# A block of attention and experts on one core: scores in four 32-row tiles, causal masks on TensorE, near values on GpSimd, products with the values in two stretches

## What is computed

```python
scores = jnp.einsum('bhqd,bhkd->bhqk', Qh, Kh)
idx = _rel_index(S, S)            # clip(k - q, -2, 2) + 2
rel_k = rel_k_table[idx]
scores = (scores + jnp.einsum('bhqd,qkd->bhqk', Qh, rel_k)) / scale
causal = jnp.tril(jnp.ones((S, S), dtype=bool))
scores = jnp.where(causal[None, None], scores, -1000000000.0)
attn = jax.nn.softmax(scores, axis=-1)
out = jnp.einsum('bhqk,bhkd->bhqd', attn, Vh)
out = out + jnp.einsum('bhqk,qkd->bhqd', attn, rel_v_table[idx])
x = x + _layernorm(out.transpose(0, 2, 1, 3).reshape(B, S, E) @ W_o + b_o)
```

## Time and profile before

| | us |
|---|---|
| median of 3 runs | 1036.85 |
| lowest, highest | 1036.38, 1038.85 |
| span of the profiled execution | 1036.5 |
| share busy in the span: PE, PEld, DVE, ACT, POOL | 86%, 50%, 80%, 65%, 70% |

### The profile page before, as it was taken

How to read it: one execution, slowest core, us unless ns; L and a number is a source line. 1 busy time by engine, 2 the same in 40 slices (tenths; PEclk the granted TensorE clock), 3 DMA queues, 4 the chain that set the end, 5 groups by cost and what they waited for, 6 DMA issues and landing times. The chain is left out here.

```text
span 1036.5 us, 23477 instructions
## 1 busy us (share of the span) xinstructions
PE 896.3 (86%) x7655; PEld 513.6 (50%) x7655; DVE 833.7 (80%) x1948; ACT 676.3 (65%) x1305; POOL 727.1 (70%) x940
## 2 busy tenths in 40 slices
PE   2778889889889898898898988986679999999995
PEld 0324444444444444444444444432457777777773
DVE  5578888888988888889888888877568788878884
ACT  2038677777676777776777777765447767676773
POOL 4135686876867868768678687576357989898886
PEclk9769999999999999999999999988889999999999
DMA  2610110110101101011011011101425455555441
GB/s 48 170 44 34 35 44 31 47 42 32 49 31 42 45 32 47 32 43 49 32 42 44 33 47 40 35 18 50 148 59 169 144 165 150 169 151 166 162 140 31
DMA packets 64004, 74.93 MB, mean 72 GB/s; under 512 B 10032, under 2 KB 39600, under 8 KB 63904
## 3 DMA queue, kind: packets, MB, share of 16 engines
q1 hardware_dynamic: 61536, 73.17, 22.4%
q10 hardware_dynamic: 2368, 0.48, 0.3%
HBM read 43.75 MB, written 8.65 MB: 51 GB/s over the span
## 5 line engine op out<-in xcount | busy, mean ns | idle before, releaser
L1128 DVE TENSOR_REDUCE mx<-ps_s 128x1 f32<-128x512 f32 (+2 forms) x640 | 408.6, 681 | 84.3 <-PE ps_s L1540 83.7
L799 ACT ACTIVATE prob<-ps_e 128x512 f32<-128x512 f32 x640 | 349.6, 606 | 103.3 <-PE ps_e L1497 103.2
L641 POOL TENSOR_SCALAR_AFFINE_SELECT prob<-prob 128x516 f32<-128x516 f32 (+1 forms) x320 | 174.9, 571 | 141.8 <-ACT prob L799 141.8
L1519 PE MATMUL ps_s<-ks,qs 63*128 63x512 f16 (+3 forms) x1024 | 224.5, 312 | 47.4 <-DVE mx L1128 31.5
L1497 PE MATMUL ps_e<-qs,ks 64*128 64x512 f16 (+3 forms) x1024 | 212.1, 307 | 3.7 <-ACT prob L799 1.7
L721 POOL TENSOR_TENSOR hidden_low<-hidden,hidden_high 128x512 fp32r<-128x512 f32 x144 | 191.1, 1356 | 12.1 <-ACT hidden_high L989 10.9
L1557 PE MATMUL ps_av<-prob,vp 128*32 128x512 f32 (+3 forms) x2048 | 182.4, 452 | 4.3 <-POOL prob L641 4.2
L1519 PEld LDWEIGHTS ps_s<-ks,qs 63*128 63x128 f16 x1024 | 67.6, 95 | 184.0 <-DVE mx L1128 80.5
L989 ACT CAST hidden_high<-hidden 128x512 fp32r<-128x512 f32 x160 | 98.0, 612 | 30.5 <-DVE hidden L1441 27.3
L1540 PE MATMUL ps_s<-masked_at,below_r 64*128 64x128 bf16 (+3 forms) x640 | 103.1, 211 | 0.0
L1540 PE MATMUL ps_s<-masked_at,below 64*128 64x128 bf16 (+3 forms) x640 | 91.3, 213 | 0.0
(11 more groups left out here) (177 smaller groups left out, 1737.7 us busy)
## 6 DMA issues: line engine op xcount, KB each, us to landing
gate_rows<-gates_dram SPq DMA_DIRECT2D x128, 256.0 KB, 3.6
qs<-qh SPq DMA_DIRECT2D x128, 32.0 KB
qs<-ql SPq DMA_DIRECT2D x128, 32.0 KB
xnT_dram<-oT SPq DMA_DIRECT2D x16, 256.0 KB, 2.0
xeT<-xnT_dram SPq DMA_DIRECT2D x16, 256.0 KB, 2.7
out<-result SPq DMA_DIRECT2D x16, 256.0 KB, 2.3
v_near<-v_back SPq DMA_DIRECT2D x16, 254.0 KB
ks<-kh SPq DMA_DIRECT2D x124, 32.0 KB
```

Source lines behind the costliest of these rows:

```text
L641: pool.affine_select(out=v, in_=v, compare_op=ALU.is_ge, fill=0.0, base=-2, pattern=cols, channel_multiplier=-1).then_inc(S["p_masked"], 1)
L799: act.activation(prob[g % 2][:, u, b, :], ps_e[bank][:, :], ACT.Exp, scale=SCALE).then_inc(S["e_done"], 1)
L1128: dve.tensor_reduce(out, src, AX.X, ALU.max).then_inc(s_free[bank], 1)
L1519: pe.matmul(scores[:, at:at + P * (qt + 1)], qs[par][rows, 2 * g + off, P * qt:P * qt + P], ks[par][rows, 2 * g + off, 0:P * (qt + 1)], st ...
```

## The change

- A tile has 32 rows: three products (low-low is gone) of 8 columns at rows 4d, 4d+1, 4d+2, the row 31 for the maxima, and three of the rows 4i+3 for a large negative product that masks the one near key across a boundary of two blocks of 128. TensorE has four tiles. E units of group g use tiles 2(g mod 2) and the next, S units run group g xor 1 and so use the other two.
- The units are cut anew: u = 0 and 3 hold the four diagonal blocks of a head, u = 1, 2 and 4 hold blocks that need no mask. A diagonal unit is four matmuls of 128 columns, and then four mask matmuls of 4 x 32 columns, for S and E alike. GpSimd masks nothing.
- Products with the values: in u = 1 the diagonal blocks of the group before (16 matmuls of 128 columns), in u = 3 the rest (widths 384, 256, 128). They wait for ScalarE's exponents (`e_done`).
- Bank v0 is read by ScalarE alone; GpSimd makes `v_back` and `v_near` from `vp` (`values_near`).
- Three pairs of stack buffers of half the size, six transfers a sequence, all in the step of stage F. One transfer for each half of the maxima in place of two. Other order of heads in `wq` and `wk`, other constants, among them six transfers that turn the mask table.

The diff, cut to its core (removed bodies are left out; they stand in the code above; the piece behind `e_part` is `s_part`):

```diff
-HALF = P // 2
-M_ROW = HALF - 1
+ROWS = 32
+M_ROW = ROWS - 1
+BIG = 65504.0
...
-E_UNITS = [[(0, 0, 0)], [(0, 1, 0), (0, 3, 384)], [(0, 2, 0), (1, 2, 256)], [(1, 0, 0)], [(1, 1, 0), (1, 3, 384)]]
-S_UNITS = [[(0, 3, 0)], [(0, 2, 0), (0, 0, 384)], [(0, 1, 0), (1, 1, 256)], [(1, 3, 0)], [(1, 2, 0), (1, 0, 384)]]
...
+def diagonal(off):
+    return [(off, t, P * t, P * t, P) for t in range(NT)]
+E_UNITS = [diagonal(0), [(0, 0, P, 0, 3 * P), (0, 2, 3 * P, 3 * P, P)], [(0, 1, 2 * P, 0, 2 * P), (1, 1, 2 * P, 2 * P, 2 * P)],
+           diagonal(1), [(1, 0, P, 0, 3 * P), (1, 2, 3 * P, 3 * P, P)]]
+S_UNITS = [diagonal(0), [(0, 3, 0, 0, 3 * P), (0, 1, 0, 3 * P, P)], [(0, 2, 0, 0, 2 * P), (1, 2, 0, 2 * P, 2 * P)],
+           diagonal(1), [(1, 3, 0, 0, 3 * P), (1, 1, 0, 3 * P, P)]]
+DIAGONAL = (0, 3)
...
+AV_AT = {1: ("diagonal",), 3: (0, 1, 2)}
+def row_tile(g, b):
+    return 2 * (g % 2) + b
+def rows_of(tile, n=ROWS):
+    return slice(ROWS * tile, ROWS * tile + n)
...
+            def stacks_out(st, s):
+                if s < 3:
+                    sp.wait_ge(S["k_rows"], 2 * (s + 1))
+                    sp.wait_ge(S["q_rows"], 2 * (s + 1))
+                for stk, parts in ((qs[s % 3], (qh, qh, ql)), (ks[s % 3], (kh, kl, kh))):
+                    if s == 0 and stk is ks[0]:
                         continue
-                    for b in range(2):
-                        for r, part in enumerate(parts):
-                            lo = 64 * b + D * r
-                            src = 64 * b + 32 * half
-                            sp.dma_start(stk[lo:lo + D, prs, :], part[src:src + 32, :]).then_inc(stacks[par][half], 16)
+                    for r, part in enumerate(parts):
...
-            def mask_tiles(st, lo, hi):
-                for g, part in ((i // NU, i % NU) for i in range(lo, hi)):
-                    last = {0: 3, 1: 3, 2: 5, 3: 9, 4: 9}[part]
...
+            def values_near(st):
+                by_head = lambda v: v.rearrange("p t (h d) -> p t h d", d=D)
+                apart = lambda i: dv[:, i, :].rearrange("p (h d) -> p h d", d=D).unsqueeze(1).to_broadcast([P, NT, H, D])
+                v = vp[st.a % 2][:, :, :, 0:D]
+                pool.wait_ge(s_free[st.s_use("v0")[1]], st.s_turn("v0") + 1)
+                need(pool, S["v_shifted"], 32 * st.a)
+                pool.tensor_tensor(by_head(v_back[:, :, :]), v, apart(0), ALU.add).then_inc(S["back_made"], 1)
+                need(pool, S["near_ready"], 4 * st.a)
+                own.mark(pool.tensor_tensor(by_head(v_near[:, 0]), v, apart(1), ALU.add))
             def near_half(st, s, half):
...
-            def values_out(st):
...
             def s_max(st, i):
-                g, u, b = i // (2 * NU), i % (2 * NU) // 2, 1 - i % 2
+                g, u, b = i // (2 * NU) ^ 1, i % (2 * NU) // 2, i % 2
                 n, bank = st.s_use(f"s{i}")
-                scores, (off, qt, _) = ps_s[bank][:, :], S_UNITS[u][0]
-                h = 2 * (2 * g + off) + b
-                if len(S_UNITS[u]) == 1:
-                    out, src = mx[:, QT0 + qt, h:h + 1], scores
+                h, n_seg = 4 * g + 2 * b + S_UNITS[u][0][0], 2 if u == 2 else NT
+                src = ps_s[bank][:, :].rearrange("p (n c) -> p n c", n=n_seg)
+                if u in DIAGONAL:
+                    out = mx[:, 0:TOP + 1:DIAG_AT, h]
                 elif u == 2:
-                    out, src = mx[:, QT0 + qt, h:h + 3:2], scores.rearrange("p (n c) -> p n c", n=2)
+                    out = mx[:, TOP + 8, h:h + 2]
                 else:
-                    out, src = mx[:, 0:QT0 + 1:4, h], scores.rearrange("p (n c) -> p n c", n=NT)
+                    out = mx[:, TOP + 1:TOP + 5, h]
...
-                own.mark(dve.tensor_reduce(mx[:, QT0 + 2, hs], mx[:, 0:QT0:4, hs].rearrange("p r h -> p h r"), AX.X, ALU.max))
+                own.mark(dve.tensor_reduce(mx[:, 3, hs], mx[:, TOP:TOP + 4, hs].rearrange("p r h -> p h r"), AX.X, ALU.max))
+                pairs = mx[:, :, hs].rearrange("p (k r x) h -> p r h k x", k=2, r=3, x=4)[:, 1:3, :, :, 0]
+                own.mark(dve.tensor_reduce(mx[:, 1:3, hs], pairs, AX.X, ALU.max))
...
             def e_part(st, i, scores, n):
                 g, u, b = i // (2 * NU), i % (2 * NU) // 2, i % 2
-                par, rows = st.b % 2, slice(HALF * b, HALF * b + HALF)
-                off, kt, at = E_UNITS[u][n]
-                pr = 2 * g + off
-                last = pe.matmul(scores[:, at:at + WIDTH[kt]], ks[par][rows, pr, P * kt:P * kt + P],
-                                 qs[par][rows, pr, P * kt:SEQ], start=True, stop=True)
-                if n == len(E_UNITS[u]) - 1:
+                rows = rows_of(row_tile(g, b))
+                off, kt, q0, at, w = E_UNITS[u][n]
+                slot = 2 * (g // 2) + off
+                last = pe.matmul(scores[:, at:at + w], ks[st.b % 3][rows, slot, P * kt:P * kt + P],
+                                 qs[st.b % 3][rows, slot, q0:q0 + w], start=(n == 0),
+                                 stop=(u not in DIAGONAL and n == len(E_UNITS[u]) - 1))
+                if u not in DIAGONAL and n == len(E_UNITS[u]) - 1:
                     last.then_inc(S["e_full"], 1)
...
+                g, u, b = i // (2 * NU) ^ 1, i % (2 * NU) // 2, i % 2
+                rows = rows_of(row_tile(g, b), M_ROW)
+                off, qt, k0, at, w = S_UNITS[u][n]
+                slot = 2 * (g // 2) + off
+                last = pe.matmul(scores[:, at:at + w], qs[st.a % 3][rows, slot, P * qt:P * qt + P],
+                                 ks[st.a % 3][rows, slot, k0:k0 + w], start=(n == 0),
+                                 stop=(u not in DIAGONAL and n == len(S_UNITS[u]) - 1))
+                if u not in DIAGONAL and n == len(S_UNITS[u]) - 1:
+                    last.then_inc(S["s_full"], 1)
+            def mask_part(bank, tile, side, part, full):
+                blocks = bank[:, :].rearrange("p (n c) -> p n c", n=NT)[:, :, ROWS * part:ROWS * part + ROWS]
+                columns = masked_at[rows_of(tile), :].unsqueeze(1).to_broadcast([ROWS, NT, ROWS])
+                last = pe.matmul(blocks, tri[rows_of(tile), (part - tile) % 4, side, :], columns,
+                                 start=False, stop=(part == 3))
+                if part == 3:
+                    last.then_inc(full, 1)
+            def av_part(st, s, g, part):
+                par, then = s % 2, st if g < NGRP - 1 else Step(st.t0 - 1)
+                if part == "diagonal":
+                    pe.wait_ge(S["e_done"], then.e_use(f"e{2 * NU * g + 7}")[0] + 1)
+                    need(pe, S["av_copied"], NGRP * s + g)
                     if g == 0:
...
+                        made = Step(st.t0 - 1)
+                        pe.wait_ge(s_free[made.s_use("v0")[1]], made.s_turn("v0") + 1)
+                    for kt in range(NT):
+                        for j in range(4):
+                            pe.matmul(ps_av[32 * j:32 * j + 32, P * kt:P * kt + P], vp[par][:, kt, 4 * g + j, :],
+                                      prob[g % 2][:, DIAGONAL[j % 2], j // 2, P * kt:P * kt + P],
+                                      start=(kt == 0), stop=False)
+                    return
+                pe.wait_ge(S["e_done"], then.e_use(f"e{2 * NU * g + 9}")[0] + 1)
                 for j in range(4):
...
+                    u, at = (2, 2 * P * (j % 2)) if part == 1 else (DIAGONAL[j % 2] + 1, 0 if part == 0 else 3 * P)
+                    w = SEQ - P * (part + 1)
+                    last = pe.matmul(ps_av[32 * j:32 * j + 32, P * (part + 1):SEQ], vp[par][:, part, 4 * g + j, :],
+                                     prob[g % 2][:, u, j // 2, at:at + w], start=False, stop=(part == 2))
+                if part == 2:
                     last.then_inc(S["av_full"], 1)
...
+                    s_banks, e_banks = [None, None], [None, None]
+                    for n in range(len(E_UNITS[u])):
+                        for b in range(2):
+                            if st.A:
+                                if n == 0:
+                                    s_banks[b] = s_unit(st, 2 * r + b)
+                                s_part(st, 2 * r + b, s_banks[b], n)
+                            if st.B:
+                                if n == 0:
+                                    e_banks[b] = e_unit(st, 2 * r + b)
+                                e_part(st, 2 * r + b, e_banks[b], n)
+                    if u in DIAGONAL:
+                        for part in range(4):
+                            for b in range(2):
+                                if st.A:
+                                    mask_part(s_banks[b], row_tile(g ^ 1, b), 0, part, S["s_full"])
+                                if st.B:
+                                    mask_part(e_banks[b], row_tile(g, b), 1, part, S["e_full"])
+                    for part in AV_AT.get(u, ()):
                         if g > 0 and st.B:
...
+                            av_part(st, st.b, g - 1, part)
```

(1 more changed line is left out.)

287 lines of the change are left out of this document (89 added, 198 removed).

## The result

| | before | after |
|---|---|---|
| median, us | 1037.85 (1036.38 to 1039.70) | 1134.61 (1126.89 to 1136.76) |
| span of the profiled execution, us | 1036.5 | 1134.9 |
| TensorE's mean granted clock | 0.960 | 0.844 |
| q matmuls to q matmuls, a step | 41.4 us | 48.0 to 50.7 us |

The changed kernel takes 1.092 times as long (95% interval 1.088 to 1.095). The forecast was 977 us.

The account below looks back on a forecast made before the run. The prediction took a step as VectorE's work plus holes from TensorE's stretches: 35.1 + 2.6 = 37.7 us, 3.7 less, 56 us over 15 steps; with 1.5 and 2 us, 59 off 1036.5 gives 977 us, range 962 to 995 (wider, 950 to 1035).

Parts of the forecast that it names:

- What bounds the kernel: Attention step of 41.41 us: VectorE's 36.03 us of work plus 5.38 us of holes torn by TensorE's stretches.
- VectorE's work: VectorE's own work in a step: 36.03 us less 1.37 plus 0.4, so 35.1 us.
- GpSimd: GpSimd loses its masks, gains the near-value additions, ends near 21.8 us a step and bounds nothing.
- The near values: Two additions moved from VectorE to GpSimd: 0.69 and 0.68 us a step off VectorE's work.
- Four tiles overlap: Scores and exponent scores in four 32-row TensorE tiles run together; a diagonal round's scores and masks take 0.58 us.
- the rival of two tiles: Only two TensorE tiles overlap, holes stay 4.66 us, a step 39.8 us: 1010 us, chance 0.17.
- the one with the starts as the limit: Rival: 654 matmul starts a step limit TensorE, a step is priced at 44 us: 1076 us, chance 0.13.
- TensorE's busy time: Scores and masks on TensorE: 1.5 us less a group, 6 us a step.
- Products with the values: Two TensorE stretches instead of three: -0.1 us a group, set against a larger hole, counted as nothing.
- What reaches the step: VectorE's seven waits a step shorten by 0.3 us each, 2.1 us; holes after, 2.6 us.
- TensorE's clock: TensorE's clock in the steps, 1.00 in five steps; a fall below full was named only as making the forecast wrong.

Follow-up runs that it names:

- order_av3: Changed kernel with products with the values in three stretches, xn2 transposed behind round 18's scores, and the maxima merged two reductions later: 1000.8 us.
- best1: order_av3 plus ten redundant TensorE matmuls a step (four in round 16, three in round 18, three in round 3): 1003.8 us.
- best1_near_dve: best1 with the two additions that make the near values back on VectorE: 1019.4 us.
- order: Changed kernel, still two stretches, with xn2 transposed behind round 18's scores and the first half's maxima merged two reductions later: 1062.3 us.
- before_two: Kernel before with its products with the values in two stretches for a group of heads instead of three, nothing else: 1115.3 us.
- fill_both: Changed kernel with 17 redundant TensorE matmuls a step where it stood idle (round 13, and before xn2's transposes in round 18): 1067.6 us.

## Why the prediction was wrong, point by point

**What bounds the kernel**: right. In every step shown above with stage C in it the length is VectorE's 34 to 36 us of work plus its idle time, most of it waits for TensorE; what differs is the holes.

**VectorE's work**, 35.1 forecast: 34.8 to 34.9 us a step in the windows above, 34.2 in order_av3. **GpSimd**, 21.8: 22.7. Both right. The near values, taken at 1.4 us a step or 22 in all, cost 15.6 on VectorE. At full clock they put 0.93 us on its work and 0.87 on a step (best1, then best1_near_dve):

```profile
314.87:354.34 39.47, 35.27 (x663) 19.82 (x659) 34.23 (x91) 30.34 (x61) 22.72 (x27) 1.00 0.11 36
239.13:279.47 40.34, 35.11 (x660) 19.91 (x659) 35.16 (x93) 30.42 (x61) 20.45 (x25) 1.00 0.11 35
```

**Four tiles overlap**: right. In a diagonal round at full clock (changed kernel, timeline of TensorE) four matmuls start within 10 ns and the next four 50 to 70 ns later, masks too:

```profile
89.67 0.22 PE L1499 MATMUL ps_s<-ks,qs 31*128 31x128 f16 x1
89.67 0.22 PE L1476 MATMUL ps_e<-qs,ks 32*128 32x128 f16 x1
89.73 0.21 PE L1499 MATMUL ps_s<-ks,qs 31*128 31x128 f16 x1
89.73 0.21 PE L1476 MATMUL ps_e<-qs,ks 32*128 32x128 f16 x1
...
89.85 0.22 PE L1509 MATMUL ps_s<-masked_at,tri 32*128 32x128 bf16 x1
89.85 0.21 PE L1509 MATMUL ps_e<-masked_at,tri 32*128 32x128 bf16 x1
```

The first two of the round's 32 matmuls stand before a wait; the other 30 start within 0.41 us (89.66 to 90.07), 14 ns each. The factor of 3.07 in place of 4, which the prediction cited from the Trainium skill ("TensorE: Matmul & The Clock Gate", "Measured speedup vs the span model"), isn't seen here: the sets of four follow each other seven times in 0.41 us, every 58 ns or so, where the prediction took 55 to 60 for a full overlap. The 62 ns for each matmul with hardware decode off (the Trainium skill, "TensorE: Matmul & The Clock Gate", "Wait — 56ns, not 53.3ns?") aren't seen either, at 14. So the rival of two tiles is out, and so is the one with the starts as the limit: it had the right sign (1076 us) for the wrong reason, since it decided from 58 ns a start. TensorE's busy time in a step at full clock fell by 4.3 us (37.4 to 33.1 in order_av3) and not by 6; where the rest went wasn't looked into.

**Products with the values**: a step that failed. The prediction saw that the later stretch grows and "tears a larger hole", set that against 0.1 us a group and counted nothing. Measured: 3.0 to 3.45 us a step at an equal clock, and 61 us (order against order_av3) to 78 us (before_two) in all. The stretch of 1.5 us and the transposes behind it (0.66 us) outlast VectorE's three banks of 0.62 us each.

**What reaches the step**: the 2.1 us a step by which the holes should shrink, since VectorE would wait less for score banks. This failed too. At an equal order, three stretches and full clock a step is 39.23 us with 34.21 of VectorE's work: 5.0 us of holes, where the kernel before has 5.38 and the forecast 2.6. VectorE's waits in three such steps (order_av3, 272.80 to 390.50 us) and TensorE's waits for ScalarE and GpSimd in them:

```profile
DVE mx L1105 <- PE ps_s L1498: 7.0, 10, 1.4
DVE mx L1105 <- PE ps_s L1508: 6.0, 6, 1.3
...
PE ps_e L1558 <- ACT qf L791: 3.1, 3, 1.0
PE ps_misc L1538 <- POOL y L617: 3.0, 3, 1.0
PE ps_e L1538 <- POOL xn L617: 2.5, 3, 0.8
...
PE ps_e L1475 <- ACT prob L769: 1.2, 3, 0.4
```

VectorE waits 4.3 us a step for score banks, as much as before (21.7 us in five steps). There are fewer waits, 5.3 a step in place of 7, and longer ones. Only the wait for bank v0 went. TensorE meanwhile waits 3.3 us a step for ScalarE and GpSimd, against 2.0 before (4.5 and 3.7 us in five steps for xn and y, 1.7 for qf). That a faster TensorE only reaches these waits earlier, and that they are what keeps VectorE's holes open, fits the numbers, but no run closes one of them alone. So even the good order is 24 us over the forecast: 1.5 us in each step at full clock, 3.3 in those with a stretch at half.

**TensorE's clock**: the largest step that failed, a term set to nothing, since all five steps stood at 1.00. The steps that begin at 210.21 and 500.47 us in the same trace don't: they stand at 0.96. The clock was named among what would make the forecast wrong, but got no price and no chance. By subtraction it is the largest part of the miss: of 158 us some 51 are the stretch at an equal clock (3.2 a step, 16 times) and 24 are what order_av3 is over the forecast, which leaves some 80 for the clock and for the two holes as such. No run parts these two; but the 67 us that fill_both gives back are the clock's, since it fills the holes without shortening them. TensorE's idle time collected in two holes of 1.7 and 2.4 us. The prediction had both waits in its rows, 0.7 us each, and wrote that "most of the time saved is time in which TensorE would stand before a full ring", without asking what such standing does. The Trainium skill has the rule: "TensorE: Matmul & The Clock Gate", "A second HAM failure mode: psum-queue depth-cycling", says that a kernel which cycles through PSUM banks can let TensorE idle briefly and often enough that its clock swings between the two levels. The trace agrees, with 0.76 to 0.86 in the steps after.

The sum of the runs: 1134.6, less 70 (three stretches), less 64 (order at the two holes), is 1000.8. The forecast had 977. Both differences hold some of the clock.
